# Projections and output products of two attentions in f32 instead of three f16 terms

## The chip, the cores and the metric

The kernel runs on one core of one Trainium2 chip. The metric is the device time of a run in microseconds, the median of three runs. A profiled execution shows where the time goes; its span runs from the first to the last instruction of the program.

## The reference, cut to what matters

The input is `x` of 4 sequences, 512 rows each, 256 columns, all f32. Six blocks follow one another, each on a layer norm of `x`:

```python
x = x + 0.5 * L0_ffn(ln(x))          # gated, 256 -> 704 -> 256, dequantised weights
x = x + L0_attn(ln(x))               # 16 heads of 16, rotary, causal
x = x + 0.5 * L0_ffn(ln(x))
x = x + 0.5 * L1_ffn(ln(x))          # gated, weights rounded to -1, 0, 1
x = x + L1_attn(ln(x))               # 16 query heads, 4 key/value heads, ALiBi, causal
x = x + 0.5 * L1_ffn(ln(x))
```

In `L0_attn`, q, k and v are `ln(x) @ W.T` with 256x256 weights; in `L1_attn`, q is `ln(x) @ Wq` (256 columns) and k and v have 64 columns each. After the softmax the context (256 columns a row) is multiplied by the output weights. All of it is f32 in the reference.

## The kernel before, in words

The work is cut into 16 feed-forward units (`FFNS`, one for each sequence and block) and 8 attention units (`ATT`, 4 sequences in 2 layers). Every engine walks through a string of letters of its own (`ORDER`), where a letter is the next step of one kind; the strings fix the order on each engine, and `banks` fixes which of the eight PSUM banks each of PE's steps writes. Between engines the steps wait on semaphores. Feed-forward steps of one sequence are interleaved with attention steps of another, so that PE nearly always has something to do.

Engines are named as in the profile: PE is TensorE (PEld its loads of the stationary operand), DVE VectorE, ACT ScalarE, POOL GpSimd, SP the queue that issues DMAs.

An attention unit goes like this. DVE and POOL form the layer norm's statistics, ACT writes the normalised rows `XN` (L776), PE transposes them into PSUM (letter `u`, L577; 8 transposes for two halves of 128 input columns). Then come the steps that matter here:

- **Rows in two f16 parts.** ACT copies a half out of PSUM as f16 (letter `y`, L789), the high part. DVE subtracts it from the PSUM value and writes the low part as f16 (letter `u` of DVE, L974). Two halves for 8 units make 16 of each.
- **Weights in two f16 parts.** Once a layer, q/k/v weights (`WA`) and output weights (`WO`) arrive by DMA in f32 in tiles that are otherwise used later (`OT`, `RB`, a part of `PB`). ACT scales them by 64 (L744) and copies them as f16 (L747), POOL subtracts (L1098) for the low part. These are letters `w` beyond the third of ACT (eight) and of POOL (four).
- **Three terms.** PE forms each product as three f16 products that add up in PSUM, high by high, high by low, low by high. `TERMS` lists them; q and k (letter `q`, L635) have 3 terms x 2 halves for a chunk of 128 output columns (`o[0:width, :]`, 512 rows as moving columns), v (letter `v`, L651) the same for each 128 rows, output (letter `o`, L719) the same for each 128 rows with 256 columns:

```python
TERMS = [(0, 0), (0, 1), (1, 0)]
for s, (jw, jx) in enumerate(TERMS):
    for k in range(2):
        m = e.matmul(o[0:width, :], WA[l][:, jw, k, ch * P:ch * P + width], XTU[1][jx][:, k, :], ...)
```

- **Scores and weighted sums.** Letters `m` and `s` form scores twice (once for the row maximum, once for the exponential), ACT takes exponentials (L846), POOL masks them (L1162), and letter `p` (L704) multiplies them with `V`. This last product is f32 in both operands already: for each of 4 blocks of keys, four calls write four groups of 32 output partitions; 16 calls a unit, 32 units.
- **Normalised context.** The sums go to `OT`; DMAs bring the context to `OC` and the row sums to `DC`, DVE takes reciprocals (L1070), DMAs spread them over `RB`. POOL multiplies (letter `c`, L1175), ACT copies to f16 (letter `c` of ACT, L862, `CH[0]`), POOL subtracts for the low part (letter `C`, L1179, `CH[1]`). Two halves for 8 units make 16 of each. Then PE does the output products and DVE adds them to `x` (L1078).

Feed-forward rows are split into two f16 parts in the same way (L783, L969), with exact f16 weights; these stay as they are. Letter `z` (L556) is filler work for PE in the first 80 us, and L564 are two f32 sums over partitions with all 128 columns and 1 or 2 moving columns.

Of the kernel before, what the change touches and what calls it, by code (L numbers as in the profile page):

```python
# [14 lines left out]
P = 128  # L15
# [13 lines left out]
WS = 64.0  # L29
# [5 lines left out]
TERMS = [(0, 0), (0, 1), (1, 0)]  # L35
# [63 lines left out]
def last_chunk(gi):  # L99
# [21 lines left out]
        "NwNtthhNhkhwwwttwhwhwwhhwwdNdwhwnwkhwuutthpqqhpwhdqdnpphqkhhhuuhtpqpqtmmmmmmxmssmmpqpqmhxhmdmmmsmmxd"  # L121
        "mhkmshnmmxmsmmhmcmmxshmmmmcmxmuummmxpqpqooNdmqppmmqmttcdmsxhsskhhsmmnmmhmmxsshhmmmmcuxudmmdNppmqmqtt"
        "ooNmxhmmhhpqkmhmmxhcpqhttsddhnksshchmmssmmmhuuxhmmsoohmmllmmxlmmdmdmmxNmmmmmxttNmhhckhmmhhhmmxttddmn"
        "sshmmkmscuusxhhhmlmssmhlhlommxmddmNmmmomxttNhhmmhkmmhcxmmhhmmmcxmmmmddnmttmmosshxuusokhlllhmmmxshssh"
        "hmmmmmxdmdmNmmmxmNcttmmchhhkhhhmmxttddnoommmNuuhmmxlllhhckmmhmmmmxmmmhmchmxmmttddmmohoxNmmhhmmmxkhch"
        "tthhhcddkhhhhooNXttddhhkhhhhdd",
    "act":
        "TwwXxxwttthwhtXthhxxtkktthhwXwwtwhhkkkttYtyyxxhhhXhtttQhvQwwwvkktYtyyQtQxhhhxhhtTQQkteeeeQtQeeehhoee"
        "eteeheeotehYoeeeteehhoeeevveeyycceoeeQeeQXoxxeeeQtQttheethhoteeeehteYoeehhcvvyyeeeecXoxxeeeeQQttthXh"
        "heettheoteexhxQhoeeeeetQhotthttvYchvyychhthQeQeeQeeeeeeeoXexxeeotetehhtthteXthhheeoxxeeettohYvttcyye"  # L130
        "eehhQtetQcehhQeheoeeeXxxeeoetteeethhheoteeXhtthhoeeveeeceecoexexYttteyyhQQQheehttethehhoeeeeeeoeeeXo"
        "exxveXttthhhtttheheheexxcceYeooyytehQQeeeQtteeeeoetXohhhvtteeeeehhxxcoceeteeehttXhheoeeteeteeeeeoxxh"
# [52 lines left out]
def macaron_kernel(nc, x_in, wqkv0, wo0, gu0, sgu0, wd0, sd0, wqkv1, wo1, gu1, wd1,  # L185
                   rope, ident, maskw, maskm, alibi_q, alibi_k, bo1, scratch, out):
    ctx = ExitStack()
    with ctx:
# [3 lines left out]
        def sem(name):  # L192
            return ctx.enter_context(nc.semaphore(name))
# [10 lines left out]
        WA = [sb(f"WA{l}", [P, 2, 2, NQKV[l]], F16) for l in range(2)]  # L204
        WO = [sb(f"WO{l}", [P, 2, 2, D], F16) for l in range(2)]
# [14 lines left out]
        XTU = [[sb(f"XT{i}{j}", [P, 2, T], F16) for j in range(2)] for i in range(2)]  # L220
# [6 lines left out]
        CH = [sb(f"CH{j}", [P, 2, T], F16) for j in range(2)]  # L227
# [31 lines left out]
        a_turn, a_xhi, a_xlo = sem("a_turn"), sem("a_xhi"), sem("a_xlo")  # L259
# [9 lines left out]
        t_rc, t_cc, t_hi, t_lo, t_bo, t_om, t_res = (sem(n) for n in ("t_rc", "t_cc", "t_hi", "t_lo", "t_bo", "t_om", "t_res"))  # L269
# [6 lines left out]
              CH[0][:, :, :].rearrange("p u t -> p (u t)").bitcast(F32).rearrange("p (c n) -> p c n", c=2)]  # L276
# [8 lines left out]
        ra = [OT[:, 0:3, :].rearrange("p g t -> p (g t)").rearrange("p (k n) -> p k n", k=2),  # L285
              raw[0][:, 4 * HID + FC * D:].rearrange("p (k n) -> p k n", k=2)]
        ro = [RB[:, l, :].rearrange("p (c n) -> p c n", c=2) for l in range(2)]
# [6 lines left out]
        XTF = [XTU[0], [spare16[:, HS0 + 2 * j * T:HS0 + 2 * j * T + 2 * T].rearrange("p (k t) -> p k t", k=2) for j in range(2)]]  # L294
# [3 lines left out]
        inv = 1.0 / (XS * WS)  # L298
# [91 lines left out]

        def wait_bank(w, c, i):

            for was in BTAB[c, i][1]:
                wait_read(w, *was)

        def wait_read(w, c, i):
# [3 lines left out]
            elif c == "u":  # L400
                w.wait_ge(a_xlo, i + 1)
# [35 lines left out]
        def sync_program(e, order):  # L437
# [10 lines left out]
            e.dma_start(ra[0], wqkv0).then_inc(l_a0, 16)  # L448
            e.dma_start(ro[0], wo0).then_inc(l_a0, 16)
# [9 lines left out]
            e.dma_start(ra[1], wqkv1).then_inc(l_a1, 16)  # L459
            e.dma_start(ro[1], wo1).then_inc(l_a1, 16)  # L460
            for c in order:
# [33 lines left out]
                elif c == "D":  # L495
# [7 lines left out]
                    w.wait_ge(t_lo, 2 * (n - 1) + u + 1)  # L503
# [8 lines left out]
                elif c == "R":  # L512
# [3 lines left out]
                    w.wait_ge(p_act, 11)  # L516
                    w.wait_ge(p_pool, 7)
# [13 lines left out]
        def tensor_program(e, order):  # L531
# [14 lines left out]
            for c in order:  # L546
# [75 lines left out]
                elif c == "q":  # L622
# [7 lines left out]
                    w.wait_ge(p_act, 7 if l == 0 else 11)  # L630
                    w.wait_ge(p_pool, 5 if l == 0 else 7)
                    for s, (jw, jx) in enumerate(TERMS):
                        for k in range(2):
                            w.wait_ge((a_xhi, a_xlo)[jx], 2 * n + k + 1)
                            m = e.matmul(o[0:width, :], WA[l][:, jw, k, ch * P:ch * P + width], XTU[1][jx][:, k, :],  # L635
                                         start=s == 0 and k == 0, stop=s == 2 and k == 1)
                    m.then_inc(a_qk, 1)
                elif c == "v":
# [68 lines left out]
                elif c == "o":  # L707

                    n, t = divmod(i, NT)
                    l = ATT[n][1]  # L710
                    if t % 2 == 0:
                        wait_bank(w, "o", i // 2)
                    o = bank("o", i // 2)
                    q = t % 2
                    w.wait_ge(p_act, 7 if l == 0 else 11)
                    w.wait_ge(p_pool, 5 if l == 0 else 7)
                    for s, (jc, jw, g) in enumerate((jc, jw, g) for jc, jw in TERMS for g in range(2)):
                        w.wait_ge((t_hi, t_lo)[jc], 2 * n + g + 1)
                        m = e.matmul(o[:, q * D:(q + 1) * D], CH[jc][:, g, t * P:(t + 1) * P], WO[l][:, jw, g, :],  # L719
                                     start=s == 0, stop=s == 5)  # L720
                    m.then_inc(t_om, 1)

        def scalar_program(e, order):
            w, at = Once(e), Counter()
            for c in order:
                i = at[c]
                at[c] += 1
                if c == "w":
# [4 lines left out]
                    elif i == 2:  # L733
                        w.wait_ge(l_d0, 16)
                        e.activation(WD[0][:, :, :], rdi, ACT.Copy, bias=-128.0).then_inc(p_act, 1)
                    else:
                        l, s = divmod(i - 3, 4)
                        if l == 0:
                            w.wait_ge(l_a0, 48)
                        else:  # L740
                            w.wait_ge(l_a1, 32)
                        src, dst = (ra[l], WA[l]) if s < 2 else (ro[l], WO[l])
                        if s % 2 == 0:
                            e.activation(src, src, ACT.Copy, scale=WS).then_inc(p_act, 1)  # L744
                        else:
                            w.wait_ge(p_act, i)
                            e.activation(dst[:, 0, :, :], src, ACT.Copy).then_inc(p_act, 1)  # L747
# [36 lines left out]
                elif c == "y":  # L784
# [4 lines left out]
                    e.activation(XTU[1][0][:, k, :], bank("u", i), ACT.Copy).then_inc(a_xhi, 1)  # L789
# [57 lines left out]
                elif c == "o":  # L847
                    n, g = divmod(i, 4)
                    w.wait_ge(a_pv, i + 1)
                    if n == 0:  # L850
                        w.wait_ge(p_act, 5)
                        w.wait_ge(p_pool, 4)
                    else:
                        w.wait_ge(t_dc[g // 2], 16 * n)
                        w.wait_ge(t_oc[g // 2], 16 * n)
                    e.activation(OT[:, g, :], bank("p", i), ACT.Copy).then_inc(a_ot, 1)
                elif c == "c":
                    n, u = divmod(i, 2)
                    w.wait_ge(t_cc, i + 1)
                    w.wait_ge(t_om, 4 * n)  # L860
                    w.wait_ge(p_dve, 14)
                    e.activation(CH[0][:, u, :], OC[:, u, :], ACT.Copy).then_inc(t_hi, 1)  # L862

        def vector_program(e, order):
# [16 lines left out]
            for c in order:  # L881
# [434 lines left out]
```

## Time and profile before

| | |
|---|---|
| median of 3 runs | 565.31 us |
| lowest, highest | 565.25, 566.36 us |
| span of the profiled execution | 563.3 us |
| instructions | 12960 |
| busy share PE, DVE, ACT, POOL | 95, 81, 71, 61% |
| DMA | 31.76 MB, mean 56 GB/s |

The profiled execution has no time of its own beside its span, which is 2.0 us below the median of the runs. A row of the profile that groups instructions gives the line, the engine, the operation, output and inputs, shapes (partitions x elements, type) and the count, then busy time and mean duration of one, then the engine's idle time before them and what ended it. The records of matmuls are pipelined, so the durations of two that follow each other overlap.

### The profile page before, as it was taken

To read this page: it belongs to the slowest core of one execution; us is meant where nothing else is said; L and a number is where in the kernel's file an instruction comes from. 1 tells how busy PE (TensorE), PEld (TensorE's weight loads), DVE (VectorE), ACT (ScalarE), POOL (GpSimd) and SP (SyncE) were. 2 spreads that over 40 slices of the span, in tenths; PEclk is the share of its full clock that TensorE was granted. 3 is DMA by queue.
4 is the path that set the end of the run, shared out by engine and by line. 5 is a ranking of instruction groups with operands and counts; after the bars stand their busy time and mean duration, and the time that the engine had idled before them with its cause. 6 is when DMAs were issued, how large, how long until landed. Compare 5 with 4: busy or idle time off the path is not lost.

```text
span 563.3 us, 12960 instructions
## 1 busy us (share of the span) xinstructions
PE 536.7 (95%) x5060; PEld 303.1 (54%) x5060; DVE 455.5 (81%) x813; ACT 400.5 (71%) x605; POOL 343.1 (61%) x427
## 2 busy tenths in 40 slices
PE   8998888999999999999899999999999999999997
PEld 7564644545554654556446564465455645654664
DVE  4799899997989698599986879878898768794453
ACT  5996675786587778765785848867778587688533
POOL 2467999855987588744456374634563735444634
PEclk9999999999999999999999999999999999999999
DMA  8800110301040102122010120010102011201201
GB/s 322 340 2 0 51 64 2 113 22 60 2 144 12 42 1 78 55 72 71 2 41 10 43 71 21 3 61 8 66 21 61 1 41 73 60 21 42 78 37 38
DMA packets 20525, 31.76 MB, mean 56 GB/s; under 512 B 7360, under 2 KB 8768, under 8 KB 20312
## 3 DMA queue, kind: packets, MB, share of 16 engines
q1 hardware_dynamic: 20464, 30.94, 15.8%
q8 instruction: 40, 0.66, 0.5%
q14 instruction: 21, 0.17, 0.1%
HBM read 13.75 MB, written 2.36 MB: 29 GB/s over the span
## 4 chain that ended last, share of the span: by engine, by line
PE 59%; DVE 15%; POOL 7%; ACT 6%; issue 5%; DMA 3%; SPq 3%; DVEq 0%; POOLq 0%; ACTq 0%
PE PS L593 16%; PE PS L704 11%; PE PS L617 9%; DVE MX L1058 5%; PE PS L669 5%; PE PS L684 4%; PE PS L635 4%; ACT PB L846 3%; PE PS L719 3%; PE PS L577 3%; DMA X<-x_in 2%; PE PS L541 2%; PE PS L651 2%; DVE ST L871 1%; DVE MX L1054 1%
## 5 line engine op out<-in xcount | busy, mean ns | idle before, releaser
L846 ACT ACTIVATE PB<-PS 128x1024 f32<-128x1024 f32 x160 | 157.2, 1024 | 50.0 <-PE PS L684 41.7
L1058 DVE TENSOR_REDUCE MX<-PS 128x2 f16<-128x1024 f32 (+2 forms) x192 | 157.7, 866 | 20.2 <-PE PS L541 19.5
L593 PE MATMUL PS<-XT,WGU 128*128 128x512 f16 x660 | 156.3, 380 | 1.7 <-ACT PB L846 0.5
L1134 POOL TENSOR_TENSOR HH<-TH,HH 128x512 f16<-128x512 f32 x71 | 82.6, 1177 | 70.4 <-ACT HH L814 70.4
L1162 POOL TENSOR_SCALAR_AFFINE_SELECT PB<-PB 128x512 f32<-128x512 f32 (+1 forms) x140 | 74.5, 560 | 69.7 <-ACT PB L846 69.7
L593 PEld LDWEIGHTS PS<-XT,WGU 128*128 128x128 f16 x660 | 59.1, 98 | 73.8 <-issue 6.2
L617 PE MATMUL PS<-WD,HH 128*128 128x256 f16 x660 | 77.3, 273 | 0.1
L704 PE MATMUL PS<-PB,V 128*32 128x512 f32 (+3 forms) x1024 | 75.5, 435 | 1.4 <-POOL PB L1162 1.1
L617 PEld LDWEIGHTS PS<-WD,HH 128*128 128x128 f16 x660 | 62.8, 98 | 11.7 <-issue 2.0
L814 ACT ACTIVATE HH<-TH 128x512 f16<-128x512 f32 (+1 forms) x86 | 52.2, 627 | 20.0 <-DVE TH L1004 7.1
L669 PE MATMUL PS<-SK,SQ 63*128 63x256 f16 (+3 forms) x512 | 58.8, 299 | 5.9 <-DVE MX L1054 2.2
L684 PE MATMUL PS<-SQ,SK 64*128 64x384 f16 (+3 forms) x512 | 54.7, 299 | 5.4 <-ACT PB L846 2.7
L704 PEld LDWEIGHTS PS<-PB,V 128*32 128x32 f32 x1024 | 31.1, 109 | 42.9 <-issue 33.2
L1004 DVE SCALAR_TENSOR_TENSOR TH<-TH,PS 128x512 f32<-128x512 f32 (+1 forms) x48 | 32.6, 686 | 21.8 <-PE PS L593 13.3
L541 PE MATMUL PS<-MASKM,MASKW 64*128 64x128 bf16 (+1 forms) x720 | 46.0, 205 | 0.0
L635 PE MATMUL PS<-XT,WA 128*128 128x512 f16 (+1 forms) x168 | 40.0, 380 | 2.5 <-DVE DS L1019 1.7
L769 ACT ACTIVATE XN<-X,OFF,YR 128x256 f32<-128x256 f32 x62 | 32.1, 590 | 12.9 <-POOL OFF L1116 12.8
L541 PEld LDWEIGHTS PS<-MASKM,MASKW 64*128 64x128 bf16 x720 | 32.5, 95 | 14.4
L871 DVE BATCH_NORM_STATS2 ST<-X 128x6 f32<-128x256 f32 x96 | 33.6, 411 | 7.7 <-DMA X<-x_in 6.3
L1054 DVE TENSOR_REDUCE MX<-PS 128x4 f16<-128x1024 f32 x32 | 39.0, 1218 | 1.0 <-PE PS L541 0.6
L669 PEld LDWEIGHTS PS<-SK,SQ 63*128 63x128 f16 x512 | 18.9, 94 | 33.0 <-issue 14.0
L684 PEld LDWEIGHTS PS<-SQ,SK 64*128 64x128 f16 x512 | 18.7, 93 | 32.1 <-issue 12.6
(117 smaller groups left out, 783.7 us busy)
## 6 DMA issues: line engine op xcount, KB each, us to landing
SQ<-QPB SPq DMA_DIRECT2D x24, 256.0 KB, 2.5
OC<-OT SPq DMA_DIRECT2D x16, 256.0 KB, 2.4
RB<-scratch SPq DMA_DIRECT2D x64, 64.0 KB, 2.2
SK<-QPB SPq DMA_DIRECT2D x12, 256.0 KB, 2.5
SQ<-MT SPq DMA_DIRECT2D x128, 1.0 KB
out<-X SPq DMA_DIRECT2D x8, 256.0 KB, 2.1
PB<-gu SPq DMA_DIRECT2D x2, 704.0 KB, 6.3
LATE<-gu SPq DMA_DIRECT2D x2, 704.0 KB, 14.6
```

The lines of the kernel that those rows point to most:

```text
L541: m = e.matmul(to, MASKW[64 * z:64 * z + 64, way, half, :], by, start=False, stop=True, skip_group_check=True)
L593: m = e.matmul(o[:, :], WGU[l][:, k, col:col + P], rows_of(f)[j][:, k, :], start=j == 0 and k == 0, stop=j == 1 and k == 1)
L617: m = e.matmul(o[:, q * D:(q + 1) * D], hidden_of(f)[j][:, s * T + t * P:s * T + (t + 1) * P], WD[l][:, s, :], start=ci == 0 and (q == 0 o ...
L635: m = e.matmul(o[0:width, :], WA[l][:, jw, k, ch * P:ch * P + width], XTU[1][jx][:, k, :], start=s == 0 and k == 0, stop=s == 2 and k == 1)
L669: e.matmul(o[:, z, col:col + kw], SQ[n % 2][64 * z:64 * z + QROWS - 1, 2 * g + pr, t * P:(t + 1) * P], SK[n % 2][64 * z:64 * z + QROWS - 1 ...
L684: m = e.matmul(o[:, z, col:col + T - kb * P], SK[n % 2][64 * z:64 * z + QROWS, 2 * g + pr if l == 0 else pr, kb * P:(kb + 1) * P], SQ[n % ...
L704: m = e.matmul(o[32 * a:32 * a + 32, kb * P:T], V[:, kb, 4 * g + a if l == 0 else a, :], PB[i % 2][:, s, a % 2, col:col + T - kb * P], sta ...
L814: e.activation(hidden_of(f)[0][0:rows, s * T:(s + 1) * T], value_of(i)[0][0:rows, :], ACT.Copy).then_inc(f_hi, 1)
L846: e.activation(PB[Q % 2][:, j, :, :], two_banks("s", i), ACT.Exp, scale=0.25).then_inc(a_exp, 1)
L1058: e.tensor_reduce(mx[:, :, pr, t], o[:, :, col:col + (t + 1) * P], AX.X, ALU.max, negate=True).then_inc(a_max, 1)
L1134: e.tensor_tensor(hh[1][:, s * T:(s + 1) * T], value_of(j)[0], hh[0][:, s * T:(s + 1) * T], ALU.subtract).then_inc(f_lo, 1)
L1162: m = e.affine_select(blk, blk, [[0, nb], [1, P]], ALU.is_ge, 0.0, base=0, channel_multiplier=-1)
```

## The change

The rows of the attentions, the weights and the normalised context are no longer split. `XTA`, `WA`, `WO` and `CH` become f32 tiles, the DMAs bring the weights straight into `WA` and `WO`, and each place with three terms becomes one product in f32. ACT writes the transposed rows to `XTA` as f32, POOL's multiply writes the context straight to `CH`. The letters `u` of DVE (16), `c` of ACT (16), `C` of POOL (16), eight `w` of ACT and four `w` of POOL are gone from the strings; nothing else in the strings has moved, and those of PE, SP and the banks are the same letter for letter. The scale of 64 is gone from weights, `inv`, the rotary table and the last multiply.

Which waits change: the three projections wait for the DMAs of the weights (`wait_projections`) and for `a_xt`; the output products wait for `t_cc`, the end of POOL's multiply; that multiply waits for the output products of the attention unit before (`t_om`), as ACT's copy did; the DMA into `OC` waits for `t_cc`.

```diff
-WS = 64.0
-TERMS = [(0, 0), (0, 1), (1, 0)]
...
-        WA = [sb(f"WA{l}", [P, 2, 2, NQKV[l]], F16) for l in range(2)]
-        WO = [sb(f"WO{l}", [P, 2, 2, D], F16) for l in range(2)]
+        WA = [sb(f"WA{l}", [P, 2, NQKV[l]]) for l in range(2)]
+        WO = [sb(f"WO{l}", [P, 2, D]) for l in range(2)]
...
-        XTU = [[sb(f"XT{i}{j}", [P, 2, T], F16) for j in range(2)] for i in range(2)]
+        XTU = [sb(f"XT0{j}", [P, 2, T], F16) for j in range(2)]
+        XTA = sb("XTA", [P, 2, T])
...
-        CH = [sb(f"CH{j}", [P, 2, T], F16) for j in range(2)]
+        CH = sb("CH", [P, 2, T])
...
-            e.dma_start(ra[0], wqkv0).then_inc(l_a0, 16)
-            e.dma_start(ro[0], wo0).then_inc(l_a0, 16)
+            e.dma_start(WA[0][:, :, :], wqkv0).then_inc(l_a0, 16)
+            e.dma_start(WO[0][:, :, :], wo0).then_inc(l_a0, 16)
...
-                    for s, (jw, jx) in enumerate(TERMS):
-                        for k in range(2):
-                            w.wait_ge((a_xhi, a_xlo)[jx], 2 * n + k + 1)
-                            m = e.matmul(o[0:width, :], WA[l][:, jw, k, ch * P:ch * P + width], XTU[1][jx][:, k, :],
-                                         start=s == 0 and k == 0, stop=s == 2 and k == 1)
+                    wait_projections(w, l)
+                    for k in range(2):
+                        w.wait_ge(a_xt, 2 * n + k + 1)
+                        m = e.matmul(o[0:width, :], WA[l][:, k, ch * P:ch * P + width], XTA[:, k, :], start=k == 0, stop=k == 1)
...
-                        for s, (jw, jx) in enumerate(TERMS):
-                            for k in range(2):
-                                m = e.matmul(o[:, (t % per) * vw:(t % per + 1) * vw], XTU[1][jx][:, k, t * P:(t + 1) * P],
-                                             WA[l][:, jw, k, v0:v0 + vw], start=s == 0 and k == 0, stop=s == 2 and k == 1)
+                        for k in range(2):
+                            m = e.matmul(o[:, (t % per) * vw:(t % per + 1) * vw], XTA[:, k, t * P:(t + 1) * P],
+                                         WA[l][:, k, v0:v0 + vw], start=k == 0, stop=k == 1)
...
-                    for s, (jc, jw, g) in enumerate((jc, jw, g) for jc, jw in TERMS for g in range(2)):
-                        w.wait_ge((t_hi, t_lo)[jc], 2 * n + g + 1)
-                        m = e.matmul(o[:, q * D:(q + 1) * D], CH[jc][:, g, t * P:(t + 1) * P], WO[l][:, jw, g, :],
-                                     start=s == 0, stop=s == 5)
+                    wait_projections(w, l)
+                    for g in range(2):
+                        w.wait_ge(t_cc, 2 * n + g + 1)
+                        m = e.matmul(o[:, q * D:(q + 1) * D], CH[:, g, t * P:(t + 1) * P], WO[l][:, g, :],
+                                     start=g == 0, stop=g == 1)
...
-                    e.activation(XTU[1][0][:, k, :], bank("u", i), ACT.Copy).then_inc(a_xhi, 1)
+                    e.activation(XTA[:, k, :], bank("u", i), ACT.Copy).then_inc(a_xt, 1)
...
-                elif c == "u":
-                    n, k = divmod(i, 2)
-                    w.wait_ge(a_xhi, i + 1)
-                    e.tensor_tensor(XTU[1][1][:, k, :], bank("u", i), XTU[1][0][:, k, :],
-                                    ALU.subtract).then_inc(a_xlo, 1)
...
-                    e.tensor_tensor(OC[:, u, :], OC[:, u, :], RB[:, u, :], ALU.mult).then_inc(t_cc, 1)
-                elif c == "C":
-                    n, u = divmod(i, 2)
-                    w.wait_ge(t_hi, i + 1)
-                    e.tensor_tensor(CH[1][:, u, :], OC[:, u, :], CH[0][:, u, :], ALU.subtract).then_inc(t_lo, 1)
+                    w.wait_ge(t_om, 4 * n)
+                    e.tensor_tensor(CH[:, u, :], OC[:, u, :], RB[:, u, :], ALU.mult).then_inc(t_cc, 1)
```

On PE, at the first output products (attention unit 0, beside q and k of unit 2), the rows stood so before:

```order
L704 MATMUL PS<-PB,V 32x128 x4
L635 MATMUL PS<-XT,WA 128x512 x12
L684 MATMUL PS<-SQ,SK 128x512 x2
L684 MATMUL PS<-SQ,SK 128x384 x2
L684 MATMUL PS<-SQ,SK 128x128 x2
L719 MATMUL PS<-WO,CH 128x256 x24
L684 MATMUL PS<-SQ,SK 128x512 x2
```

And so in the change, where L704, L635, L684 and L719 have become L701, L636, L681 and L715:

```order
L701 MATMUL PS<-PB,V 32x128 x4
L636 MATMUL PS<-XTA,WA 128x512 x4
L681 MATMUL PS<-SQ,SK 128x512 x2
L681 MATMUL PS<-SQ,SK 128x384 x2
L681 MATMUL PS<-SQ,SK 128x128 x2
L715 MATMUL PS<-WO,CH 128x256 x8
L681 MATMUL PS<-SQ,SK 128x512 x2
```

Nothing has moved; there is one product for three, twelve of q and k have become four, and 24 of the output eight.

On POOL, at the context of the last attention unit (`OC`, `CH`) among low parts of feed-forward values (`HH`), the rows stood so before:

```order
L1162 AFFINE_SELECT PB<-PB 128x4x128
L1134 TENSOR_TENSOR HH<-TH,HH 128x512 x3
L1175 TENSOR_TENSOR OC<-OC,RB 128x512
L1179 TENSOR_TENSOR CH<-OC,CH 128x512
L1134 TENSOR_TENSOR HH<-TH,HH 128x512
L1175 TENSOR_TENSOR OC<-OC,RB 128x512
L1134 TENSOR_TENSOR HH<-TH,HH 128x512
L1179 TENSOR_TENSOR CH<-OC,CH 128x512
L1134 TENSOR_TENSOR HH<-TH,HH 128x512 x3
```

And so in the change (L1097 for L1134, L1139 for L1175):

```order
L1125 AFFINE_SELECT PB<-PB 128x4x128
L1097 TENSOR_TENSOR HH<-TH,HH 128x512 x3
L1139 TENSOR_TENSOR CH<-OC,RB 128x512
L1097 TENSOR_TENSOR HH<-TH,HH 128x512
L1139 TENSOR_TENSOR CH<-OC,RB 128x512
L1097 TENSOR_TENSOR HH<-TH,HH 128x512 x4
```

Both subtractions are gone; the multiply writes `CH` itself, and a low part of the feed-forward that stood between the second multiply and its subtraction now joins the three behind it.

## Rows read from the trace of the kernel before

**Rows 1.** The page: busy us, share, instructions; clock by slice.

```profile
PE 536.7 (95%) x5060; PEld 303.1 (54%) x5060; DVE 455.5 (81%) x813; ACT 400.5 (71%) x605; POOL 343.1 (61%) x427
...
PEclk9999999999999999999999999999999999999999
```

**Rows 2.** Stretches: length, busy PE, PEld, DVE, ACT, POOL (count), clock.

```profile
50.00:100.00 50.00, 43.95 (x326) 24.77 (x326) 46.47 (x77) 34.08 (x56) 46.84 (x43) 1.00 0.09 33
100.00:560.50 460.50, 447.39 (x4446) 248.15 (x4440) 370.64 (x642) 329.05 (x494) 270.01 (x349) 1.00 0.13 44
sum 547.50, PE 525.74 PEld 294.11 DVE 449.65 ACT 394.22 POOL 340.12; mean PE 175.25 PEld 98.04 DVE 149.88 ACT 131.41 POOL 113.37
```

**Rows 3.** The page's chain of waits, shares by engine and line.

```profile
PE 59%; DVE 15%; POOL 7%; ACT 6%; issue 5%; DMA 3%; SPq 3%; DVEq 0%; POOLq 0%; ACTq 0%
PE PS L593 16%; PE PS L704 11%; PE PS L617 9%; DVE MX L1058 5%; PE PS L669 5%; PE PS L684 4%; PE PS L635 4%; ACT PB L846 3%; PE PS L719 3%; PE PS L577 3%; DMA X<-x_in 2%; PE PS L541 2%; PE PS L651 2%; DVE ST L871 1%; DVE MX L1054 1%
```

**Rows 4.** Groups by line and shape: busy us, mean ns | idle before.

```profile
L635 PE MATMUL PS<-XT,WA 128*128 128x512 f16 x144 | 34.2, 380 | 2.5 <-DVE DS L1019 1.7 <-DVE MX L1058 0.6
L719 PE MATMUL PS<-WO,CH 128*128 128x256 f16 x192 | 23.2, 273 | 0.1
L651 PE MATMUL PS<-WA,XT 128*128 128x256 f16 x96 | 11.7, 273 | 0.0
L635 PE MATMUL PS<-XT,WA 128*64 128x512 f16 x24 | 5.9, 383 | 0.0
L651 PE MATMUL PS<-WA,XT 128*128 128x64 f16 x96 | 3.5, 193 | 0.0
```

**Rows 5.** The chain in order of time: start us, us, what and count.

```profile
223.85 1.29 PE PS L635 x6
...
381.95 1.31 PE PS L719 x12
...
424.41 0.70 PE PS L651 x24
```

**Rows 6.** f32 on PE: a group, two pieces of chain, one stretch of timeline.

```profile
L704 PE MATMUL PS<-PB,V 128*32 128x512 f32 x256 | 34.1, 604 | 1.4 <-POOL PB L1162 1.1 <-ACT PB L846 0.2
...
448.12 2.29 PE PS L704 x32
...
387.97 0.87 PE PS L577 x8
...
43.16 0.38 PE L564 MATMUL PS<-GS,LATE 128*128 128x2 f32 x2 [0.97 <-ACT TH L802]
...
43.41 0.38 PE L593 MATMUL PS<-PB,WGU 128*128 128x512 f16 x1
```

**Rows 7.** Groups of loads of the stationary operand, f16 and f32.

```profile
L635 PEld LDWEIGHTS PS<-XT,WA 128*128 128x128 f16 x144 | 12.9, 98 | 19.6 <-DVE DS L1019 2.0 <-issue 1.9 <-DVE MX L1058 1.0
L577 PEld LDWEIGHTS PS<-ID,XN 128*128 128x128 f32 x192 | 21.3, 140 | 8.1 <-DVE MX L1058 1.7 <-issue 1.5 <-ACT XN L776 1.0
L564 PEld LDWEIGHTS PS<-GS,LATE 128*128 128x128 f32 x4 | 0.7, 189 | 1.4 <-ACT TH L802 1.2
```

**Rows 8.** Groups of removed instructions.

```profile
L974 DVE TENSOR_TENSOR XT<-PS,XT 128x512 f16<-128x512 f32 x16 | 10.3, 683 | 4.2 <-ACT XT L789 4.0
L862 ACT ACTIVATE CH<-OC 128x512 f16<-128x512 f32 x16 | 10.1, 633 | 8.6 <-POOL OC L1175 8.6
L1179 POOL TENSOR_TENSOR CH<-OC,CH 128x512 f16<-128x512 f32 x16 | 18.4, 1162 | 4.5 <-ACT CH L862 4.5
```

**Rows 9.** The chain in order of time, about 251 us and about 535 us.

```profile
250.91 0.27 DVE XT L974
251.42 0.68 DVE XT L974
...
534.63 1.13 POOL CH L1179
...
535.81 2.26 PE PS L719 x19
```

More of the change, by code:

```diff
@@ new lines @@
+        "shnmmxmsmmhmcmmxshmmmmcmxmmmmxpqpqooNdmqppmmqmttcdmsxhsskhhsmmnmmhmmxsshhmmmmcxdmmdNppmqmqttooNmxhmm"
+        "hhpqkmhmmxhcpqhttsddhnksshchmmssmmmhxhmmsoohmmllmmxlmmdmdmmxNmmmmmxttNmhhckhmmhhhmmxttddmnsshmmkmscs"
+        "xhhhmlmssmhlhlommxmddmNmmmomxttNhhmmhkmmhcxmmhhmmmcxmmmmddnmttmmosshxsokhlllhmmmxshsshhmmmmmxdmdmNmm"
+        "mxmNcttmmchhhkhhhmmxttddnoommmNhmmxlllhhckmmhmmmmxmmmhmchmxmmttddmmohoxNmmhhmmmxkhchtthhhcddkhhhhooN"
+        "Xttddhhkhhhhdd",
+    "act":
+        "TwwXxxwttthhtXthhxxtkktthhXthhkkkttYtyyxxhhhXhtttQhvQvkktYtyyQtQxhhhxhhtTQQkteeeeQtQeeehhoeeeteeheeo"
+        "tehYoeeeteehhoeeevveeyyeoeeQeeQXoxxeeeQtQttheethhoteeeehteYoeehhvvyyeeeeXoxxeeeeQQttthXhheettheoteex"
+        "hxQhoeeeeetQhotthttvYhvyyhhthQeQeeQeeeeeeeoXexxeeotetehhtthteXthhheeoxxeeettohYvttyyeeehhQtetQehhQeh"
+        "eoeeeXxxeeoetteeethhheoteeXhtthhoeeveeeeeoexexYttteyyhQQQheehttethehhoeeeeeeoeeeXoexxveXttthhhtttheh"
+        "eheexxeYeooyytehQQeeeQtteeeeoetXohhhvtteeeeehhxxoeeteeehttXhheoeeteeteeeeeoxxhthohtthhtthththhXxxtht"
+        "thththhth",
@@ L139 @@
+        "ceffffhhhhhffbddfffrrhhhhhccffeffrffbfffhhhhhccfrffhhffffffhhhchchhhhrhhhhh",
     "banks":
@@ L268, in macaron_kernel @@
         t_dc, t_oc, t_so, t_si = ([sem(f"t_{n}{u}") for u in range(2)] for n in ("dc", "oc", "so", "si"))
-        t_rc, t_cc, t_hi, t_lo, t_bo, t_om, t_res = (sem(n) for n in ("t_rc", "t_cc", "t_hi", "t_lo", "t_bo", "t_om", "t_res"))
+        t_rc, t_cc, t_bo, t_om, t_res = (sem(n) for n in ("t_rc", "t_cc", "t_bo", "t_om", "t_res"))
         o_out = sem("o_out")
@@ L293, in macaron_kernel @@
         HHU = [HH0, [spare16[:, 0:FC * T], spare16[:, FC * T:HS0]]]
-        XTF = [XTU[0], [spare16[:, HS0 + 2 * j * T:HS0 + 2 * j * T + 2 * T].rearrange("p (k t) -> p k t", k=2) for j in range(2)]]
+        XTF = [XTU, [spare16[:, HS0 + 2 * j * T:HS0 + 2 * j * T + 2 * T].rearrange("p (k t) -> p k t", k=2) for j in range(2)]]
         T0 = (HS0 + 4 * T) // 2
         BEFORE = {FC * ND + (r - FC * ND) % 3: max(j for j in range(FC * ND) if j % 5 == r) for r in range(3)}
-        inv = 1.0 / (XS * WS)
+        inv = 1.0 / XS
         def hidden_of(f):
@@ L389, in wait_lo, with wait_projections @@
                 w.wait_ge(f_lo, (FC - 1) * f + ci)
+        def wait_projections(w, l):
+            if l == 0:
+                w.wait_ge(l_a0, 48)
+            else:
+                w.wait_ge(l_a1, 32)
         def wait_bank(w, c, i):
@@ L400, in wait_read @@
             elif c == "u":
-                w.wait_ge(a_xlo, i + 1)
+                w.wait_ge(a_xt, i + 1)
             elif c == "G":
@@ L732, in scalar_program @@
                         e.activation(WGU[0][:, i, :], rgui[:, i, :], ACT.Copy, bias=-128.0).then_inc(p_act, 1)
-                    elif i == 2:
+                    else:
                         w.wait_ge(l_d0, 16)
                         e.activation(WD[0][:, :, :], rdi, ACT.Copy, bias=-128.0).then_inc(p_act, 1)
[L736 to L747, printed above, removed]
                 elif c == "k":
@@ L849, in scalar_program @@
                     w.wait_ge(a_pv, i + 1)
[L850 to L855, printed above, removed]
-                    e.activation(OT[:, g, :], bank("p", i), ACT.Copy).then_inc(a_ot, 1)
-                elif c == "c":
-                    n, u = divmod(i, 2)
[L859 to L862, printed above, removed]
+                    w.wait_ge(t_dc[g // 2], 16 * n)
+                    w.wait_ge(t_oc[g // 2], 16 * n)
+                    e.activation(OT[:, g, :], bank("p", i), ACT.Copy).then_inc(a_ot, 1)
         def vector_program(e, order):
```

58 lines of the change are left out of this document (13 added, 45 removed).

## The prediction

> **What bounds the kernel now.** I read the page first [rows 1]. TensorE (PE) is busy for 95% of the span, VectorE (DVE) for 81%, ScalarE (ACT) for 71% and GpSimd (POOL) for 61%, and the granted clock is full in every slice (2.4 GHz). A busy share says little by itself, so the busy times by stretch come next [rows 2]. Between 13 us, when PE has work for good, and its end it is idle for 547.5 - 525.7 = 21.8 us. Of these 6.1 us lie in the 50 us from 50 to 100 us, where DVE is busy for 46.5 and POOL for 46.8 of 50 us: there the others set the pace. From 100 us on PE is idle for 13.1 of 460.5 us. A matmul's record runs about 0.17 us past its streaming, so shorter waits are hidden in this: some more slack exists than these 21.8 us, but not much. The chain of waits [rows 3] agrees: PE carries 59% of it, and the three groups of products that the change touches carry 4% (q and k, L635), 3% (output, L719) and 2% (v, L651). This is a kernel that PE's stream bounds, except between 50 and 100 us.
>
> **The price of the three f16 terms.** One product of a 512-column f16 operand takes 1.29 / 6 = 215 ns, of 256 columns 1.31 / 12 = 109 ns, and with 64 columns 0.70 / 24 = 29 ns [rows 5]. By the counts of [rows 4], there are 28 units of q and k (144 + 24 records, 6 in each): 36.1 us; 192 output products in 16 pairs of 12: 21.0 us; the v products are 96 of 256 columns (8 units, 10.5 us) and 96 of 64 columns (4 units, 2.8 us). Sum 70.4 us of streaming.
>
> **The price of f32.** The kernel has f32 products already, the weighted sums of v (L704). There every call left two records (32 units of 16 calls, 1024 records), and a record of 512 columns lasts 604 ns against 380 ns in f16: 224 ns more, another pass of 215. So a call is two loads of the stationary operand and four passes. The unit's total agrees: four column groups run side by side (256 records of 604 ns fit in 34.1 us), and 2 records x 1280 columns x 2 passes x 0.42 ns is 2.15 us of the measured 2.29 us [rows 6]. Taken over to all 128 columns, one f32 call of 512 columns costs 4 x 215 = 0.86 us. Four passes take the place of three:
> - q and k: 28 units of 2 calls, 1.72 us for 1.29: **+12.0 us**.
> - output: 16 pairs of 4 calls of 256 columns, 4 x 4 x 0.108 = 1.73 us for 1.31: **+6.7 us**.
> - v, layer 0: 8 units of the same size: **+3.4 us**.
> - v, layer 1: 8 calls of 64 columns make 16 records, and here the load decides. Two passes of 64 columns would be 55 ns. But an f32 load of 128 columns lasts 189 ns against 98 in f16 [rows 7], and the one place with such loads and almost no columns (L564, two records of 2 columns, 43.16 to 43.41 us) shows 125 ns a record; the f32 transposes with 128 columns run at 0.87 / 8 = 109 ns [rows 6]. I take 109, since a stream of 16 is nearer to the eight transposes than to a lone pair: 1.74 us for 0.70, **+4.2 us** (bounds +0.7 and +5.2).
> - In the other units the load hides under the stream before it (109 ns of load, 216 or 430 ns of stream), save at a unit's head. 56 units (28 + 16 + 12) times at most 189 - 98 = 91 ns is 5.1 us, at least 0; most heads follow other streams, so I take a quarter, **+1.3 us**.
>
> PE's stream grows by 27.6 us.
>
> The Trainium skill ("TensorE: Matmul & The Clock Gate", section "Weight-path perf modes") says that fast weight load is off for FP32. That speaks against this change; by it the loads of 98 and 189 ns are what is to be expected, and the layer-1 v units should be bound by loads as costed above.
>
> **What is removed elsewhere** [rows 8]. DVE loses 16 low parts of the rows (L974, 10.3 us); ACT loses 16 high parts of the context (L862, 10.1 us), POOL their 16 low parts (L1179, 18.4 us). The weights have 768, 256, 384 and 256 columns in two halves, 3328 in all, which ACT went over twice and POOL once: by the 633 and 1162 ns that the same engines take for 512 columns, an estimate of 8 us on ACT and 7.5 on POOL. The copies that remain (rows out of PSUM on ACT, the context's multiply on POOL) have the same 128x512 size and keep their price, f32 for f16 output. None of this is the bound, and PE's order is untouched, so it shortens only waits. On the chain itself lie 0.95 us of L974 and 1.13 us of L1179 [rows 9]: **-2.1 us**. The latter is the last unit's context, whose low part PE awaits until 535.81. Of a stall that goes there, PE's own longer stream is late next. One wait moves: the multiply on POOL now waits for the output products of the unit before (ACT's copy did). Behind it in POOL's queue are masks and low parts. A whole unit of scores, exponentials and sums lies between the two, so I cost it at nothing; if those products were late, the masks and through them the weighted sums would wait. The loads of the weights go straight to their tiles and are as large as before: nothing.
>
> **The sum.** Not all of the 27.6 us reaches the end. About a sixth of it (by PE's order eight units of q and k and two of v, 8 x 0.43 + 2 x 0.42 = 4.3 us) lies between 50 and 100 us, where PE is not the bound; I count that as absorbed. Of the rest 2.1 us is given back on the chain, and I allow 1.2 us for short waits on DVE and ACT that shrink. 27.6 - 4.3 - 2.1 - 1.2 = +20.0 us. A cross-check from the chain: the touched groups have 4, 3 and 2% of 563.3 us there, 22.5, 16.9 and 11.3 us of their 36.1, 21.0 and 13.3, so 62, 80 and 85% of their growth lies on the old chain at once: 7.5 + 5.4 + 6.4 = 19.3, less 2.1, 17.2 us as a near lower bound. The profiled execution spans 563.3 us, the median of the runs is 565.3, 2.0 above it; I add to the median: **585.3 us**.
>
> **Rivals.**
> 1. *Everything lands.* PE has no slack between 50 and 100 us either, since its queue is in order and later work moves with it, and each head of a unit pays its full load: 27.6 + 3.8 + 1.0 (layer-1 v at 125 ns) - 2.1 = +30: 595.6 us. For: PE idles 12% of that stretch at most. Against: DVE and POOL are busier there than PE. Chance 0.13.
> 2. *The relief pays.* Waits on DVE and ACT shrink by the visible 21.8 us nearly whole while the added work fills them: +27.6 - 2.1 - 15 = about +10, 575 us. For: DVE and ACT lose 10 and 17 us. Against: PE's waits are spread in short pieces and move along with PE. Chance 0.09.
> 3. *Loads are not hidden.* An f32 load waits until the matmul before it has streamed. Outside layer-1 v that is 304 f32 records (112 + 128 + 64), each 109 ns longer, 33 us more: 585.3 + 33 = 618 us. The transposes speak against it, with a 140 ns load and a period of 109 ns for two passes of 128 columns or less [rows 6, 7]. Chance 0.03. The Trainium skill ("TensorE: Matmul & The Clock Gate", section "Part 3: Packing small matmuls — row/col tiling") has this rule, that a load overlaps a matmul in flight only in another row group; by that rule f16 products too would show their load of 98 ns beside the stream, and the 109 ns a product of 256 columns leave no room for it.
> 4. *Faster: a call over all 128 columns is one record of two passes.* The pair of records at L704 could belong to its four narrow column groups. Then two passes replace three: q and k -12.0, output -6.7 and v layer 0 -3.4 us, v layer 1 +0.2, together -22; with 80% on the chain and 2.1 us on top, -20: 545 us. It decides at the first q unit: 0.86 us instead of 1.72. Against it: L564 has all 128 columns and left two records for each of its calls too. Chance 0.04.
>
> **The numbers.** Forecast (579 to 592 us) 0.70, rivals 0.13, 0.09, 0.03, 0.04, and 0.01 for no difference. About 0.2% is what a measurement here tells from no change. The range of 8 in 10 leaves out rivals 3 and 4 and the outer ends of 1 and 2: 577 to 597. Faster 0.04, same 0.01, slower 0.95.
>
> **What would show it.** Right: L635's successor in groups of 4 records with 600 ns mean and about 1.7 us a unit; PE's busy time up by some 25 us, its share at 96 to 97%, DVE's share down to 77%; layer-1 v at about 110 ns a record; the idle time of PE between 50 and 100 us smaller. Wrong: one record a call; units of q above 1.9 us (loads not hidden); or PE's busy time up by 26 us with the span up by less than 12, which would mean that waits held more than the records show.

## The result and the profile after

The changed kernel takes 588.18 us (median of 4 runs, 586.72 to 589.5) against 565.4 us beside it, 1.0395 of the kernel before with an interval of 1.0372 to 1.0419. A second set on another occasion gave 587.66 against 564.46 us, 1.0412 (1.0394 to 1.0429). It is 22.8 us slower (23.2 in the second set); the forecast was 20.0 us slower, with a range that holds the measured time. Of the four executions two, of 586.72 and 587.83 us, had a mean granted clock of 1.0, and two, of 588.54 and 589.5 us, one of 0.997; the profile is of the first. No ratio counts an execution of the kernel with one term that took 2214.62 us.

First the page of the changed kernel, its part on busy times, the clock, and the chain of waits by engine and line, which answer to [rows 1] and [rows 3]:

```profile
span 585.0 us, 12502 instructions
...
PE 562.6 (96%) x4876; PEld 319.0 (55%) x4876; DVE 447.3 (76%) x797; ACT 388.2 (66%) x581; POOL 318.3 (54%) x407
...
PEclk9999999999999999999999999999999999999999
...
PE 75%; DVE 12%; ACT 5%; issue 3%; POOL 2%; DMA 1%; SPq 0%; DVEq 0%; ACTq 0%; POOLq 0%
PE PS L596 19%; PE PS L701 12%; PE PS L620 11%; PE PS L636 9%; PE PS L666 5%; PE PS L681 5%; PE PS L715 5%; DVE MX L1027 4%; PE PS L648 4%; ACT PB L830 4%; PE PS L580 3%; PE PS L544 2%; DVE ST L845 2%; DMA X<-x_in 1%; POOL PB L1125 1%
```

PE's busy time rose by 25.9 us and the span by 21.7. PE carries 75% of the chain where it carried 59%; the three touched groups (now L636, L715, L648) carry 9, 5 and 4% where they carried 4, 3 and 2. The clock is as before. DVE, ACT and POOL are less busy by 8.2, 12.3 and 24.8 us; how little this was worth is tested below.

Then the stretches of the changed kernel (length, then busy PE, PEld, DVE, ACT and POOL), which answer to [rows 2]:

```profile
50.00:100.00 50.00, 46.62 (x292) 26.05 (x292) 44.15 (x73) 31.14 (x50) 44.39 (x40) 1.00 0.09 33
100.00:582.00 482.00, 470.28 (x4292) 262.28 (x4288) 364.88 (x630) 323.22 (x479) 251.84 (x333) 1.00 0.13 42
sum 569.00, PE 551.73 PEld 310.04 DVE 441.23 ACT 381.75 POOL 315.33; mean PE 183.91 PEld 103.35 DVE 147.07 ACT 127.25 POOL 105.11
```

Between 50 and 100 us PE's idle time shrank from 6.1 to 3.4 us. After 100 us it shrank only from 13.1 to 11.7 us.

The groups of the changed kernel by line and shape (busy us, mean ns), which answer to [rows 4] and [rows 7]:

```profile
L636 PE MATMUL PS<-XTA,WA 128*128 128x512 f32 x96 | 45.3, 606 | 0.6 <-DVE MX L1027 0.6
L715 PE MATMUL PS<-WO,CH 128*128 128x256 f32 x128 | 30.1, 383 | 0.0
L715 PEld LDWEIGHTS PS<-WO,CH 128*128 128x128 f32 x128 | 23.7, 190 | 4.2 <-issue 0.9
L648 PE MATMUL PS<-WA,XTA 128*128 128x256 f32 x64 | 15.4, 386 | 0.0
L648 PE MATMUL PS<-WA,XTA 128*128 128x64 f32 x64 | 7.9, 276 | 0.0
L636 PE MATMUL PS<-XTA,WA 128*64 128x512 f32 x16 | 7.7, 605 | 0.0
```

Every call left two records with 604 to 606 ns for 512 columns, as the weighted sums did. Group by group, the busy time of q and k went from 34.2 + 5.9 to 45.3 + 7.7 us (+12.9), of the output products from 23.2 to 30.1 (+6.9), of v from 11.7 + 3.5 to 15.4 + 7.9 (+8.1). That is +27.9 us where the forecast had +27.6 for the stream. PE's busy time as a whole rose by 25.9 only, since records of different groups overlap at their ends.

The chain of the changed kernel in order of time shows single units (start us, us, what, records), which answer to [rows 5]:

```profile
214.17 1.91 PE PS L636 x4
230.81 1.72 PE PS L636 x4
...
339.32 1.73 PE PS L715 x8
...
440.24 1.73 PE PS L648 x16
```

A unit of q takes 1.72 us where it streams at once and 1.91 us where its first load is not hidden. Output products take 1.73 us a pair with loads of 190 ns, so these are hidden under a stream of 216 ns. The last row is v of layer 1: 16 records of 64 columns in 1.73 us, 108 ns each (in the trace most of them start 112 ns after the one before), where two passes would be 55 ns. This agrees with the cost by the load of 128 f32 columns; the f32 transposes, which load as many, run at 109 ns.

### The profile page after: what moved, and what is told of

It reads as the page before. It is cut to its first block, busy times and chain, and to the rows that moved or that the text cites. A ratio compares the mean times of both kernels' runs of the same rounds, so it can differ in the third digit from the quotient of the medians.

```text
span 585.0 us, 12502 instructions
## 1 busy us (share of the span) xinstructions
PE 562.6 (96%) x4876; PEld 319.0 (55%) x4876; DVE 447.3 (76%) x797; ACT 388.2 (66%) x581; POOL 318.3 (54%) x407
## 4 chain that ended last, share of the span: by engine, by line
PE 75%; DVE 12%; ACT 5%; issue 3%; POOL 2%; DMA 1%; SPq 0%; DVEq 0%; ACTq 0%; POOLq 0%
PE PS L596 19%; PE PS L701 12%; PE PS L620 11%; PE PS L636 9%; PE PS L666 5%; PE PS L681 5%; PE PS L715 5%; DVE MX L1027 4%; PE PS L648 4%; ACT PB L830 4%; PE PS L580 3%; PE PS L544 2%; DVE ST L845 2%; DMA X<-x_in 1%; POOL PB L1125 1%
## 5 line engine op out<-in xcount | busy, mean ns | idle before, releaser
L1097 POOL TENSOR_TENSOR HH<-TH,HH 128x512 f16<-128x512 f32 x71 | 82.6, 1175 | 84.1 <-ACT HH L798 84.1
L701 PE MATMUL PS<-PB,V 128*32 128x512 f32 (+3 forms) x1024 | 75.5, 435 | 1.4 <-POOL PB L1125 1.0
L620 PEld LDWEIGHTS PS<-WD,HH 128*128 128x128 f16 x660 | 62.8, 98 | 11.7 <-issue 2.0
L681 PE MATMUL PS<-SQ,SK 64*128 64x384 f16 (+3 forms) x512 | 54.5, 299 | 5.3 <-ACT PB L830 2.7
L701 PEld LDWEIGHTS PS<-PB,V 128*32 128x32 f32 x1024 | 30.9, 109 | 42.9 <-issue 33.0
L636 PE MATMUL PS<-XTA,WA 128*128 128x512 f32 (+1 forms) x112 | 52.9, 606 | 0.6 <-DVE MX L1027 0.6
L681 PEld LDWEIGHTS PS<-SQ,SK 64*128 64x128 f16 x512 | 18.6, 93 | 33.8 <-issue 14.1
```

The source lines that it names most:

```text
L620: m = e.matmul(o[:, q * D:(q + 1) * D], hidden_of(f)[j][:, s * T + t * P:s * T + (t + 1) * P], WD[l][:, s, :], start=ci == 0 and (q == 0 o ...
L636: m = e.matmul(o[0:width, :], WA[l][:, k, ch * P:ch * P + width], XTA[:, k, :], start=k == 0, stop=k == 1)
L681: m = e.matmul(o[:, z, col:col + T - kb * P], SK[n % 2][64 * z:64 * z + QROWS, 2 * g + pr if l == 0 else pr, kb * P:(kb + 1) * P], SQ[n % ...
L701: m = e.matmul(o[32 * a:32 * a + 32, kb * P:T], V[:, kb, 4 * g + a if l == 0 else a, :], PB[i % 2][:, s, a % 2, col:col + T - kb * P], sta ...
L1097: e.tensor_tensor(hh[1][:, s * T:(s + 1) * T], value_of(j)[0], hh[0][:, s * T:(s + 1) * T], ALU.subtract).then_inc(f_lo, 1)
```

## The experiments

All of them compare with the kernel before on the same chip.

**A fourth f16 term.** This kernel has four passes for each product of q, k, v and output, as the change has, but without f32 and without any relief ("relief" is the work that the change takes off DVE, ACT and POOL). The index that marks the last product of a sum moves with `TERMS`, here and in the other runs with another number of terms.

```diff
-TERMS = [(0, 0), (0, 1), (1, 0)]
+TERMS = [(0, 0), (0, 1), (1, 0), (1, 1)]
```

> The kernel before with a fourth f16 term (low by low) in every q, k, v and output product; nothing else differs. PE's stream grows by 28 x 2 x 0.215 + 8 x 4 x 0.109 + 16 x 4 x 0.109 + 4 x 8 x 0.029 = 23.4 us, with no relief of DVE, ACT and POOL and no f32 loads. Theory A (the growth of PE's stream lands, less what is absorbed while other engines set the pace): 583 to 588 us, that is 18 to 23 us over the kernel before. Theory B (the growth lands whole and the 22 us of the change are 27 us less about 5 us that the removed instructions gave back): 588 to 590 us here. Theory C (f32 itself costs more than its passes: loads, changes between types): 575 to 582 us here.

584.07 us against 564.45, ratio 1.0346 (1.0329 to 1.0362): +19.6 us for 23.4 us of stream. Theory A holds. B and C fall: 23.4 us of plain f16 passes cost 19.6 us with no relief. The change adds 27.6 - 23.4 = 4.2 us more to the stream by the forecast and cost 3.2 us more (3.6 in its second set). The loads of v in layer 1 and at the heads of units account for this difference; f32 has no large further price.

**Two terms.** For q, k and v the low part of the weights is left out of the products. The output products read the pairs of `TERMS` the other way round (context first), so what they leave out is the low part of the context, not of the weights as the expectation says. PE then no longer waits for POOL's subtraction of the context, though POOL still does it.

```diff
-TERMS = [(0, 0), (0, 1), (1, 0)]
+TERMS = [(0, 0), (0, 1)]
```

> The kernel before without its third f16 term (low part of weights or of output weights), so these products leave a part out. PE's stream shrinks by 23.4 us. Theory A (PE's stream is the bound nearly everywhere): 543 to 549 us. Rival (DVE, ACT and POOL stand close behind PE, and take over at once): 551 to 558 us, with PE's idle time up by more than 10 us.

561.52 us, ratio 0.9948 (0.993 to 0.9966): 23.4 us less stream gave 2.9 us. Both expectations were too low; the rival was nearer, and PE's idle time did grow by more than 10 us, as it said. The page of this kernel:

```profile
span 559.6 us, 12592 instructions
...
PE 518.6 (93%) x4876; PEld 286.8 (51%) x4876; DVE 455.2 (81%) x813; ACT 399.9 (71%) x605; POOL 342.6 (61%) x427
...
PE 44%; DVE 19%; POOL 11%; ACT 10%; issue 8%; DMA 5%; SPq 3%; DVEq 0%; POOLq 0%; ACTq 0%
```

PE's share of the chain falls to 44%, and its idle time grows from 26.6 us (563.3 - 536.7) to 41.0 us (559.6 - 518.6). The kernel before stands at a bend: more work on PE is paid for the most part, less is hardly rewarded.

**Where the growth lands.** Three steps of PE mark the way: the first product of q, the start of the first weighted sums and the start of the last ones. The rows are from the timeline (start us, us, engine, line, shapes, records), first the kernel before:

```profile
50.26 1.95 PE L635 MATMUL PS<-XT,WA 128*128 128x512 f16 x7
...
104.58 0.64 PE L704 MATMUL PS<-PB,V 128*32 128x512 f32 x4
...
518.33 1.07 PE L704 MATMUL PS<-PB,V 128*32 128x512 f32 x8
```

the changed kernel:

```profile
49.44 2.74 PE L636 MATMUL PS<-XTA,WA 128*128 128x512 f32 x6
...
104.93 1.06 PE L701 MATMUL PS<-PB,V 128*32 128x512 f32 x8
...
539.43 1.06 PE L701 MATMUL PS<-PB,V 128*32 128x512 f32 x8
```

the changed kernel once more, from another execution (its times stand further below):

```profile
50.23 2.31 PE L636 MATMUL PS<-XTA,WA 128*128 128x512 f32 x5
...
105.73 1.06 PE L701 MATMUL PS<-PB,V 128*32 128x512 f32 x8
...
540.33 1.06 PE L701 MATMUL PS<-PB,V 128*32 128x512 f32 x8
```

and with four terms:

```profile
50.30 1.95 PE L635 MATMUL PS<-XT,WA 128*128 128x512 f16 x7
...
105.88 1.06 PE L704 MATMUL PS<-PB,V 128*32 128x512 f32 x8
...
537.45 1.06 PE L704 MATMUL PS<-PB,V 128*32 128x512 f32 x8
```

The two traces of the changed kernel, which is one program, differ by 0.8 us at the first product of q already, before any product that the change touches. So a start at one step says little, and only the stretches between steps can be compared (us):

| trace | first q to first sums | first to last sums |
|---|---|---|
| before | 54.32 | 413.75 |
| changed, and once more | 55.49, 55.50 | 434.50, 434.60 |
| four terms | 55.58 | 431.57 |
| two terms | 54.30 | 411.46 |

In the first stretch the changed kernel and four terms both give PE 4.3 us more to do and take 1.2 and 1.3 us longer: about 3.1 us are absorbed, with the relief and without it alike. In the second stretch they lose 20.8 and 17.8 us. By the starts of PE's steps (from the first record of one line to the first of the next) the touched products take 23.1 and 18.7 us more there, and its other steps, with the waits in them, 2.3 and 0.9 us less. So waits past 105 us give back about a tenth of the growth in the changed kernel and a twentieth with four terms. Behind the last sums both lose another 0.5 to 0.6 us.

**The removed work put back.** In the changed kernel, at the old places of the orders and waited for, with values unchanged:

```diff
+                elif c == "u":
+                    k = i % 2
+                    w.wait_ge(a_xt, i + 1)
+                    e.tensor_tensor(XTA[:, k, :], bank("u", i), XTA[:, k, :], ALU.max).then_inc(a_xlo, 1)
...
+                elif c == "c":
+                    u = i % 2
+                    w.wait_ge(t_cc, i + 1)
+                    e.activation(CH[:, u, :], CH[:, u, :], ACT.Copy).then_inc(t_hi, 1)
...
+                elif c == "C":
+                    u = i % 2
+                    w.wait_ge(t_hi, i + 1)
+                    e.tensor_tensor(OC[:, u, :], OC[:, u, :], CH[:, u, :], ALU.subtract).then_inc(t_lo, 1)
```

> The changed kernel with instructions of the removed sizes put back at their old places in the orders and waited for as before, with no effect on the values: 16 on DVE after the copy of the rows, 16 on ACT and 16 on POOL after the context's multiply; only the weight conversions stay away. Theory A (the relief was worth little, PE hides it): 588 to 590.5 us, at most 2 us over the changed kernel. Theory B (the relief gave back about 5 us): 592 to 594 us.

588.75 us against 564.45, ratio 1.0426 (1.0409 to 1.0443). The changed kernel again:

> The changed kernel once more, beside the kernels below on the same chip: 1.037 to 1.042 of the kernel before. It is the base for the next run.

587.66 us against 564.46, ratio 1.0412 (1.0394 to 1.0429). The two ratios differ by 0.0014, that is 0.8 us for 16 instructions on each of DVE, ACT and POOL together, and their intervals overlap: no effect is shown, and one of more than some 2 us is ruled out. Theory A holds and Theory B (592 to 594 us) falls.

The trace shows where something may be lost. PE starts its first product of q at 50.91 us, held up by the instruction put back on DVE:

```profile
50.91 1.53 PE L604 MATMUL PS<-XTA,WA 128*128 128x512 f32 x3 [0.24 <-DVE XTA L920]
```

The kernel before had no such wait at this place. Its first term needs the high parts alone, and PE began at 50.26 us while DVE was still at both low parts:

```profile
49.83 1.29 DVE L974 TENSOR_TENSOR XT<-PS,XT 128x512 f16<-128x512 f32 x2 [1.03 <-ACT XT L789]
```

So putting the steps back is stricter here than what was removed. From the first to the last weighted sums this kernel takes 435.06 us, 0.5 us more than the changed one.

**DVE's part alone**, the first piece of the diff above:

> The changed kernel with the 16 instructions of DVE alone put back after the copy of the rows (0.68 us each) and waited for, with no effect on the values. The chart of the run with both put back showed 1.4 us lost before the first weighted sums end (107 us) and 0.5 us after. Theory A (DVE's relief counts only in the first 107 us, where PE is not alone at the bound): 0.8 to 1.6 us over the changed kernel. Rival (the context's steps before the output products were what counted): under 0.5 us over it.

588.71 us, ratio 1.0432 (1.0415 to 1.0449), 1.05 us over the changed kernel on the same chip. The number is Theory A's, but it isn't shown that DVE's instructions cost it. All four executions of this kernel (588.64 to 589.55 us) had a mean granted clock of 0.997; of those of the changed kernel beside it three had 1.0 (587.24 to 587.73 us) and one 0.997, and this one took 588.48 us. In the trace the clock was lower just ahead of the first product of q (length, then busy PE, PEld, DVE, ACT and POOL, then the clock):

```profile
45.00:52.00 7.00, 5.48 (x18) 3.17 (x19) 5.74 (x10) 5.75 (x11) 4.30 (x7) 0.76 0.00 1
```

For a part of this stretch the granted clock was at the lower of its two levels (1.2 GHz and not 2.4), after PE had waited in pieces of up to 0.6 us. The trace of the changed kernel has the same pieces and a clock of 1.00 there. The 1.4 us of the expectation, too, were counted from the trace of the changed kernel that was 0.8 us ahead before anything differs. Past the first q, this kernel takes 55.68 us to the first sums and 434.81 us on to the last, 0.2 us more each than the changed one. So neither the size nor the place of DVE's relief is shown; with the context's steps put back as well, the time was the same (588.75 us).

**f32 for the output products alone.** Rows, q, k and v stay in three terms; `CH` and `WO` are as in the changed kernel.

```diff
-                    for s, (jc, jw, g) in enumerate((jc, jw, g) for jc, jw in TERMS for g in range(2)):
-                        w.wait_ge((t_hi, t_lo)[jc], 2 * n + g + 1)
-                        m = e.matmul(o[:, q * D:(q + 1) * D], CH[jc][:, g, t * P:(t + 1) * P], WO[l][:, jw, g, :],
-                                     start=s == 0, stop=s == 5)
+                    for g in range(2):
+                        w.wait_ge(t_cc, 2 * n + g + 1)
+                        m = e.matmul(o[:, q * D:(q + 1) * D], CH[:, g, t * P:(t + 1) * P], WO[l][:, g, :],
+                                     start=g == 0, stop=g == 1)
```

> Only the context and the output weights are f32; rows, q, k, v stay in three f16 terms. PE's stream grows by 6.7 us; ACT loses 10.1 us, POOL 18.4 us, and the chain POOL, ACT, POOL before the output products is one step. Theory A: 569 to 572 us (about 4 to 6.5 over the kernel before, a little less than the stream's growth since no part of it lies between 50 and 100 us but 1 to 2 us of chain go). Rival (the shorter chain pays for the passes): 563 to 567 us, no change or faster.

572.13 us, ratio 1.0132 (1.0117 to 1.0147): +7.7 us where A had 4 to 6.5. All of the 6.9 us of stream lands and nothing comes back, though POOL and ACT lost 28 us of work and the path to the output products lost two steps. The rival falls clearly. It is some 0.8 us over the stream, which is about the half width of the interval (0.0015 of 564 us); by the starts of PE's steps 0.4 us of it lies at steps that the edit doesn't touch, and why stays open.

One wait has moved in this kernel as in the changed one: POOL's multiply waits for the output products of the unit before. It cost nothing that shows. In the changed kernel all of POOL's idle time before this multiply is ended by DMAs:

```profile
L1139 POOL TENSOR_TENSOR CH<-OC,RB 128x512 f32<-128x512 f32 x16 | 20.2, 1270 | 13.2 <-DMA RB<-scratch 13.2
```

**Two terms, rows and context by their high parts alone.** High by high and high rows by low weights; the low parts of rows and context are left out, with the instructions that made them and PE's waits for them. Its output products are the same as in the run with two terms.

```diff
-TERMS = [(0, 0), (0, 1), (1, 0)]
+TERMS = [(0, 0), (1, 0)]
...
-                elif c == "u":
-                    n, k = divmod(i, 2)
-                    w.wait_ge(a_xhi, i + 1)
-                    e.tensor_tensor(XTU[1][1][:, k, :], bank("u", i), XTU[1][0][:, k, :],
-                                    ALU.subtract).then_inc(a_xlo, 1)
...
-                elif c == "C":
-                    n, u = divmod(i, 2)
-                    w.wait_ge(t_hi, i + 1)
-                    e.tensor_tensor(CH[1][:, u, :], OC[:, u, :], CH[0][:, u, :], ALU.subtract).then_inc(t_lo, 1)
...
-                    for s, (jc, jw, g) in enumerate((jc, jw, g) for jc, jw in TERMS for g in range(2)):
-                        w.wait_ge((t_hi, t_lo)[jc], 2 * n + g + 1)
+                    for s, (jc, jw, g) in enumerate((jc, jw, g) for jw, jc in TERMS for g in range(2)):
+                        w.wait_ge(t_hi, 2 * n + g + 1)
```

> The kernel before with two f16 terms of another kind: high part times high part and high rows (or context) times low weights. The low parts of the attention rows and of the context are left out, with the 16 subtractions on DVE and the 16 on POOL that made them. PE's stream is as in the run with two terms (23.4 us less), DVE does 10.3 us less and POOL 18.4 us less. Theory D (with PE's stream shorter the others bound, so their relief pays now): 553 to 557 us, 5 us or more under the run with two terms. Rival (what binds there are waits of single chains through ACT's exponentials, not the load of DVE and POOL): 559 to 562 us.

557.28 us, ratio 0.987 (0.9853 to 0.9888): 7.2 us under the kernel before and 4.2 us under the other kernel with two terms, which has the same PE stream. Its mean granted clock was no higher (0.996 and 0.997 in its four executions, 0.996 to 1.0 in the other's), so the clock doesn't make the difference. From the first to the last weighted sums it takes 407.37 us against 411.46, so all of the 4 us is gained there. The relief that shows no clear effect beside four passes is worth 4 us beside two: Theory D's direction, with a little less than its size. What was removed is work on DVE and POOL and also PE's wait for DVE's low parts; which of them gave the 4 us is not separated, so the expectation's rival, waits of single chains, isn't excluded. Its page:

```profile
span 556.0 us, 12554 instructions
...
PE 518.9 (93%) x4876; PEld 287.1 (52%) x4876; DVE 444.7 (80%) x797; ACT 400.0 (72%) x605; POOL 325.0 (58%) x411
```

This is the lowest median of these runs, at the price of f16 rows and contexts in these products; the kernel with one term, next, can't be told from it.

**One term.** All low parts are left out, those of the weights and POOL's four subtractions too; orders and waits are otherwise those of the run before.

```diff
-TERMS = [(0, 0), (0, 1), (1, 0)]
+TERMS = [(0, 0)]
```

> The kernel before with the high parts alone, one f16 product for each; all low parts in these products are left out, those of the weights on POOL too. PE's stream is 46.8 us shorter than in the kernel before (a third of three terms each time). Theory D: 545 to 553 us, with the gain beyond the run before this one small, since DVE and ACT bind. Rival (PE binds still): 530 to 540 us.

Ratio 0.9888 (0.9857 to 0.9918), three executions from 556.81 to 559.93 us, so both expectations were too low. The profile is of the execution of 2214.62 us and isn't read. Another 23.4 us off PE's stream gave nothing beyond the kernel with two terms and the high parts of rows and context: PE's stream is not the bound there. What is, no run shows.

## Why the prediction was right, point by point

- **Two loads and four passes a call, taken over from the narrow products to 128 columns: right.** 606 ns a record, 1.72 us a q unit, 1.73 us an output pair. Rival 4 (one record of two passes) is out. (Its term for v of layer 1, +0.2 us, is that of one unit; four make +0.7, which moves its 545 us by half a microsecond.)
- **v of layer 1 bound by its loads, 109 ns a record: right.** 108 ns measured at a unit on the chain, +1.03 us a unit where +1.04 was costed.
- **Loads hidden elsewhere: right**, rival 3 is out. A head that isn't hidden costs 0.19 us (1.91 against 1.72). The f16 units had such heads too, 1.40 against 1.29 us in the chain before, so f32 adds 0.08 us a head, under the 91 ns taken as the most. The sum over the groups came to +27.9 for +27.6.
- **4.3 us absorbed between 50 and 100 us: right in place, too large in size.** About 3.1 us were absorbed between the first q and the first weighted sums, and as much with four terms, so this has nothing to do with the relief. PE's idle time from 50 to 100 us shrank by 2.7 us.
- **-2.1 us on the chain and -1.2 us for shrinking waits: over-sized as well.** Past 105 us waits gave back 2.3 us of 23.1, and 0.9 of 18.7 with no relief at all. Putting the steps back costs 0.8 us by the ratios, which is not clear of noise, so most of the 2.1 us for L974 and L1179 on the old chain was no gain: with PE's stream longer these steps had slack. In the output-only kernel the two steps before the output products are gone as well and the whole stream landed.
- **What is removed elsewhere.** POOL's busy time fell by 24.8 us where 18.4 + 7.5 were forecast, ACT's by 12.3 where 10.1 + 8 were. Neither is the bound, so the sum doesn't depend on it. The wait that moved on POOL cost nothing, as forecast.
- **Whole sum.** Forecast 27.6 - 4.3 - 3.3 = 20.0. By the starts of PE's steps 4.3 + 23.1 + 0.5 = 27.9 us were added and 3.1 + 2.3 taken back, which makes 22.5 us. The medians say 22.8 and 23.2 us. The span of the first profile grew by 21.7 us, because that execution was 0.8 us ahead at the first q; the span of the second grew by 22.6 (585.9 us). So the cost was right, and what is absorbed or given back was put at 7.6 us and was 5.4. The cross-check's lower bound of 17.2 us holds, but isn't near.
- **Rival 1 (all lands) was nearer the truth after 105 us**, where nine tenths of the growth landed; it is wrong in the first stretch. Rival 2 (relief pays) is out: it took 15 us for what shows as 0.8 us.

## What to carry to other kernels

In these traces an f32 product over 128 columns is four passes and two loads of 190 ns (0.86 us for 512 moving columns, where three f16 terms take 0.65), so on an engine that bounds the kernel it costs more than the three terms it replaces. Count the passes from an f32 product that the trace already shows, and let the load decide where there are few moving columns, as the 64 of v in layer 1. Removing work from the other engines did not pay here for work added to the bound; the test is to put it back at the same places, with no stricter waits than before, and to compare executions of the same granted clock. The share of one engine in the chain of waits tells how the time answers neither to more work nor to less: here 23.4 us more of PE cost 19.6 us and 23.4 us less gave 2.9 us.

## What was not expected

- The bend is sharp. By the chain PE held 59%; the runs show 0.84 us for each us of stream added (four terms) and 0.12 for each us removed (two terms).
- The idle time of PE says little about what more work it can take in: after 100 us the kernel before had 13.1 us of it, and 1.4 us of that went in the change (2.3 by the starts of PE's steps, since the records hide short waits).
- The two kernels with two terms, equal in PE's stream, differ by 4.2 us through 32 instructions on DVE and POOL and the wait for them. Where PE's stream was longer, 48 instructions put back cost 0.8 us, within noise.
- Two executions of one program differed by 0.8 us before the first touched product, as much as the effects that were looked for. A stretch between two steps repeated to 0.1 us.
